# Routed rows of a mixture of experts written to their tokens' places by an indirect DMA per tile, in three groups of sequences

## The reference

```python
shared_out = einsum('tsh,shd->td', silu(xf @ sw1) * (xf @ sw3), sw2)
logits = xf @ router_w.T + experts_bias
rw, sel = top_k(logits, 2);  rw = softmax(rw)
cw = (one_hot(sel, 8) * rw[..., None]).sum(axis=1)
eo = silu(einsum('td,edh->teh', xf, w1)) * einsum('td,edh->teh', xf, w3)
moe_out = einsum('te,teh,ehd->td', cw, eo, w2)
x = layernorm(x + moe_out + shared_out)
```

## Time and profile before

| | us |
|---|---|
| median of 3 runs (615.56 to 618.25) | 616.53 |
| the profiled execution | 615.48 |
| its span | 613.5 |
| TensorE matmul, weight load busy | 500.8, 335.3 |
| VectorE busy | 467.0 |
| ScalarE busy | 313.0 |
| GpSimd busy | 323.5 |

### The profile page before, as it was taken

The page is one execution under the profiler, slowest core; times in us unless marked ns, Lnnn a source line. Parts: engine busy times, 40 slices in busy tenths (PEclk is TensorE's granted clock), DMA queues, the critical chain, the costliest instruction groups (busy, mean ns, idle before and its releaser), DMA issues.

```text
span 613.5 us, 14589 instructions
## 1 busy us (share of the span) xinstructions
PE 500.8 (82%) x4278; PEld 335.3 (55%) x4278; DVE 467.0 (76%) x1938; ACT 313.0 (51%) x752; POOL 323.5 (53%) x533
## 2 busy tenths in 40 slices
PE   6568889899879789999999989999899985497300
PEld 3212344456544249856675666767568984497200
DVE  3498999999978886998898999999826872165334
ACT  3106766766646645566666746575774432153100
POOL 5405634834668730268646765366865456405254
PEclk9786999999979789999999999999999998699755
DMA  5863322042526147744756483572456575697111
GB/s 167 230 199 113 115 80 80 3 130 80 165 72 191 57 127 210 247 144 140 230 166 188 128 238 104 139 212 90 127 149 183 159 215 142 183 306 244 39 52 51
DMA packets 77390, 90.40 MB, mean 147 GB/s; under 512 B 10241, under 2 KB 59393, under 8 KB 77313
## 3 DMA queue, kind: packets, MB, share of 16 engines
q1 hardware_dynamic: 69616, 78.79, 43.0%
q0 software_dynamic: 4096, 8.40, 4.6%
q10 hardware_dynamic: 3600, 2.30, 1.4%
HBM read 67.16 MB, written 21.89 MB: 145 GB/s over the span
## 4 chain that ended last, share of the span: by engine, by line
PE 55%; DVE 17%; issue 10%; POOL 4%; ACT 4%; DMA 4%; SPq 3%; another core or an unknown queue 2%; ACTq 0%; POOLq 0%; DVEq 0%
PE ps L1229 16%; PE ps L1135 10%; PE ps L1241 9%; PE ps L1091 8%; DVE sums L1311 6%; POOL yg L904 3%; PE ps L1077 2%; DVE acc L1459 2%; ACT probs L948 2%; PE ps L1146 2%; PE ps L1213 2%; DVE negmax L1311 1%; SPq L801 1%; PE ps L1084 1%
## 5 line engine op out<-in xcount | busy, mean ns | idle before, releaser
L1311 DVE CUSTOM_DVE_ANT_0 sums<-ps,mask_sb 128x384 bf16<-128x384 f32 (+3 forms) x512 | 218.0, 483 | 28.3 <-PE ps L1091 27.6
L948 ACT ACTIVATE probs<-ps 128x512 f32<-128x512 f32 x320 | 171.4, 610 | 54.5 <-PE ps L1091 44.9
L882 POOL TENSOR_SCALAR_AFFINE_SELECT probs<-probs 128x256 f32<-128x256 f32 (+1 forms) x320 | 113.0, 365 | 115.8 <-ACT probs L948 108.1
L1091 PE MATMUL ps<-stack 64*128 64x512 bf16 (+3 forms) x1024 | 120.2, 314 | 25.5 <-DMA stack<-parts_scratch 7.5
L1229 PE MATMUL ps<-xgT,w_tile 128*128 128x128 f32 x736 | 99.7, 284 | 0.8 <-ACT ot L984 0.6
L1436 DVE SCALAR_TENSOR_TENSOR gate<-th,ps 128x256 f32<-128x256 f32 x124 | 51.5, 416 | 63.3 <-ACT th L1012 55.8
L1229 PEld LDWEIGHTS ps<-xgT,w_tile 128*128 128x128 f32 x736 | 90.4, 196 | 9.1 <-issue 6.8
L904 POOL DMA_INDIRECT yg<-rows_out,slot x64 | 61.5, 961 | 60.2 <-DVE acc L1459 25.0
L1091 PEld LDWEIGHTS ps<-stack 64*128 64x128 bf16 x1024 | 42.7, 96 | 83.9 <-issue 21.2
L1135 PE MATMUL ps<-probs,va 128*32 128x512 f32 (+3 forms) x1024 | 84.0, 473 | 5.0 <-POOL probs L882 3.4
L894 POOL DMA_INDIRECT rows_in<-x,slot x64 | 63.0, 984 | 35.1 <-DVE slot L1428 23.9
(11 more groups left out here) (108 smaller groups left out, 582.6 us busy)
## 6 DMA issues: line engine op xcount, KB each, us to landing
w_tile<-in_experts SPq DMA_DIRECT2D x92, 384.0 KB
stack<-parts_scratch SPq DMA_DIRECT2D x106, 128.0 KB
parts_scratch<-parts SPq DMA_DIRECT2D x16, 384.0 KB
xg<-rows_in SPq DMA_DIRECT2D x20, 256.0 KB
rows_out<-y_routed SPq DMA_DIRECT2D x69, 64.0 KB
rows_in<-zeros SPq DMA_DIRECT2D x14, 192.0 KB, 3.8
x_t<-in_x SPq DMA_DIRECT2D x8, 256.0 KB, 3.0
x_r<-in_x SPq DMA_DIRECT2D x8, 256.0 KB
```

Of the source, the lines that this page charges most:

```text
L882: pool.affine_select(out=area, in_=area, compare_op=ALU.is_ge, fill=0.0, base=0, pattern=pattern, channel_multiplier=-1).then_inc(masked, 1)
L948: act.activation(probs[:, (s * NB + v) % PRING, :], bank("scores", s, v), ACT.Exp, scale=SCALE)\
L1091: return pe.matmul(into[:, at:at + width], here[:, stationary, at_s:at_s + P], here[:, moving, at_m:at_m + width], start=True, stop=True)
L1311: ins = dve.tensor_tensor_reduce(sums[:, use % 2, at:at + w], bank("max", s, u)[:, at:at + w], mask_sb[:, S - w:S], -1.0, 3.0e38, ALU.add, ...
```

## The change

Three groups, of three, three and two sequences: 31, 31 and 23 tiles. The scattered rows get two more columns: the place of the token and rank 0's expert. The sorted rows bring them back with each tile. `destinations` (VectorE, once per load of four tiles) compares the tile's expert with the row's first expert and so gets the row in `rows_out` where it belongs: token by token, both ranks side by side. `put_rows` then scatters each finished tile there with one indirect DMA from GpSimd's queue; padding rows have a place past the bound and are dropped. The stores from SP's and ScalarE's queues and the 64 gathers are gone. `load_y` fetches one sequence's 1024 rows (512 KB) with one plain DMA from SP's queue, once all puts of its group have landed and the combine before is done. There are seven weight buffers in place of eight, and the planner's tables are other ones: gaps between indirect DMAs go from 2600 and 1300 ns to 1300 and 1000, HOLD from 1000 to 500.

```diff
-SORTED = [[0, 1], [2, 3], [4, 5], [6, 7]]
+SORTED = [[0, 1, 2], [3, 4, 5], [6, 7]]
...
-GAP, GAP_LAST, GAP_END = 2600, 1300, 0
-HOLD = 1000
+GAPS = dict(scatter=(1300, 1000), put=(1000, 1000))
+HOLD = 500
...
-    XRING, WRING, YRING, HRING, TRING = 3, 8, 4, 3, 3
+    XRING, WRING, YRING, HRING, TRING = 3, 7, 4, 3, 3
...
+            if kind == "dest":
+                return [("sp", "load_rows", s, key[1])] + [("sp", "load_y", n) for n in (SORTED[s - 2] if s >= 2 else ())]
...
+            if kind == "put":
+                _, g, k = STEP[s]
+                found = [("act", "down", s), ("dve", "dest", g, k // XQ)]
+                return found + [("sp", "load_y", n) for n in (SORTED[g - 2] if g >= 2 else ())]
...
+        if kind == "load_y":
+            g = group_of[s]
+            found = [("pool", "put", step_of[("routed", g, k)]) for k in range(TILES[g])]
+            return found + [("dve", "combine", s - 1, T)]
...
-        x1 = sb("x1", [P, X1RING, T, D]); x1T = sb("x1T", [P, 2, S])
+        x1 = sb("x1", [P, X1RING, T, D + 2]); x1T = sb("x1T", [P, 2, S])
...
-        reached = sb("reached", [1, NT, E]); expert_f = sb("expert_f", [1, NT]); expert = sb("expert", [1, 2, NT], I32)
+        reached = sb("reached", [P, NT, E]); expert_f = sb("expert_f", [P, 2, NT]); expert = sb("expert", [1, 2, NT], I32)
...
-        def store_rows(eng, i):
...
-            eng.dma_start(rows_out[g % 2][k * P:(k + 1) * P, :], y_routed[:, use % YRING, :])\
-              .then_inc(rows_stored[use % YRING], 16)
...
+                    sp.wait_ge(dest_done, dest_use[(gone, qone)] + 1)
                     sp.wait_ge(*filled("T", gone, min(XQ * qone + XQ, TILES[gone]) - 1))
...
+            def load_y(s):
+                g = group_of[s]
+                for n in range(YRING):
+                    sp.wait_ge(rows_stored[n], 16 * stores_of(n, g))
+                if s > 0:
+                    sp.wait_ge(combined, s)
+                r0 = 2 * S * SORTED[g].index(s)
+                sp.dma_start(yg[:, :, :, :].rearrange("p t r d -> p t (r d)"),
+                             rows_out[g % 2][r0:r0 + 2 * S, :].rearrange("(t p r) d -> p t (r d)", p=P, r=2))\
+                  .then_inc(gathered[s % 2], 16)
...
-            def gather(g, s, t, r):
...
+            def put_rows(i):
...
+                pool.wait_ge(*drained("down", i))
+                pool.wait_ge(dest_done, dest_use[(g, k // XQ)] + 1)
+                if i == first_put[g] and g >= 2:
+                    for s in SORTED[g - 2]:
+                        pool.wait_ge(gathered[s % 2], 16 * (s // 2 + 1))
                 pool.indirect_dma_start(
-                    out=yg[:, t, r, :], out_offset=None, in_=rows_out[g % 2],
...
+                    out=rows_out[g % 2][0:count, :], out_offset=bass.IndirectOffsetOnAxis(ap=dest[:, g % 2, k:k + 1], axis=0),
+                    in_=y_routed[:, use % YRING, :], in_offset=None, bounds_check=count - 1, oob_is_err=False)\
+                    .then_inc(rows_stored[use % YRING], 16)
...
+                dve.tensor_copy(x1[:, s % X1RING, :, D], column["mark"][:, s * T:s * T + T])
+                dve.tensor_copy(x1[:, s % X1RING, :, D + 1], topf[:, :, 0])
...
+            def destinations(g, q):
...
+                dve.wait_ge(rows_here[use % XRING], 16 * (use // XRING + 1))
+                if g >= 2:
+                    for s in SORTED[g - 2]:
+                        dve.wait_ge(gathered[s % 2], 16 * (s // 2 + 1))
+                link(dve.tensor_tensor(same[:, 0:n], xg[:, use % XRING, 0:n, D + 1], expert_f[:, g % 2, XQ * q:XQ * q + n],
+                                       ALU.is_equal), dest_chain, 2 * done + 1)
+                link(dve.scalar_tensor_tensor(out=dest_f[:, 0:n], in0=same[:, 0:n], scalar=-1.0, in1=xg[:, use % XRING, 0:n, D],
+                                              op0=ALU.mult, op1=ALU.add), dest_chain, 2 * done + 2)
+                dve.tensor_scalar(dest[:, g % 2, XQ * q:XQ * q + n], dest_f[:, 0:n], float(past + 1), None, ALU.add)\
+                   .then_inc(dest_done, 1)
```

More of the change, by code:

```diff
@@ L395, in needs @@
                 rows = range(T) if key[1] == T else key[1:]
-                return [("pool", "gather", group_of[s], s, t, r) for t in rows for r in range(2)] + \
-                       [("pool", "shared_rows", step_of[("shared", s, t)]) for t in rows] + [("dve", "weights", s, 0)]
+                return [("sp", "load_y", s)] + [("pool", "shared_rows", step_of[("shared", s, t)]) for t in rows] + [("dve", "weights", s, 0)]
             if kind == "ln2_stats":
@@ L462, in length, with gap_of @@
         return round(taken), round(lasts)
+    def gap_of(part):
+        g = STEP[part[2]][1] if part[1] == "put" else part[2]
+        return GAPS[part[1]][g == len(SORTED) - 1]
     def plan():
@@ L505, in plan @@
                     continue
-                if kind in ("scatter", "gather"):
-                    after = GAP if part[2] < len(SORTED) - 1 else GAP_LAST if kind == "scatter" else GAP_END
+                if kind in GAPS:
+                    after = gap_of(part)
                     if now < indirect + after:
@@ L640, in build_block @@
         column = {}
[L641 removed]
+        for name, wide in (("earlier", P), ("ones", P), ("iota", E), ("thr", MOST), ("below", E), ("upto", E), ("tile", NT * E), ("mark", B * T)):
             column[name] = consts_sb[:, at:at + wide]
```

167 lines of the change are left out of this document (76 added, 91 removed), and 8 rows, old and new, of the table LATER.

## The result

The change makes the kernel slower: 641.7 us (640.7 to 646.4, four runs) against 617.0 us, a ratio of 1.042 (95% interval 1.036 to 1.047). The forecast was 599.6 us. The profiled execution took 640.7 us with a span of 638.9.

What follows compares the result with a forecast made beforehand. TensorE and VectorE bound the attention, then latency chains, last tiles and gathers. Last group's start 3.7 us earlier, last tiles equal, tail 12.2 shorter: span 613.5 - 15.9 = 597.6, so 599.6 us; range 585 to 616.

Steps and rivals of the forecast that it cites:

- the price of a put: TensorE idle per indirect DMA beside tiles: at most 0.16 us from 476 to 510 us, 0.54 where gathers are back to back.
- The attention: Up to the last output projection: 16 us from postponed tiles less 5 net, so 11 to 12 us earlier, at 464.
- forecast price of a tile: During attention, from 58 tiles in 50 us beyond five sequences' 240 us: 0.86 us a routed tile.
- the start: Kernel's start: more fills and tables cost 0 to 3 us, left at nothing in the sum.
- VectorE's new instructions: During attention: 0.6 us for each of 12 loads of sorted rows, 7 us, plus 3 us for two copies a sequence.
- The stretch behind the attention: Last output projection to last group's first tile: puts among scatters on GpSimd make it 8.4 us longer, first tile at 525.
- The last tiles: Last group's 23 tiles: 45 us kept; puts cost 3.7 us, set against 3.2 of gathers; clock near 1.0, some 2 us.
- The tail: Behind the last tile: put, two 512 KB loads, combines, norms and output take 27.3 in place of 39.5 us.
- C: Rival: indirect DMAs beside tiles hold TensorE's results, 0.54 us each, 626 us; decides from 0.46 us a put; chance 0.11.
- D: Rival: a put outlasts the tile period; at 1.9 + 0.3 us the last 23 tiles take 12.4 longer, 612; chance 0.04.
- wrong if above 474: Sign: sequence 7's last output projection near 464 us; above 474, VectorE or holds took the gain.
- Left at nothing: Effects priced at zero: rows of 520 bytes, one weight buffer less, SP's loads behind puts, more fills and tables.

Runs made afterwards that it cites:

- first kind: Three sets of runs in which the kernel before takes 616 to 619 us and traces show waits ended by "remote"; changed kernel 1.036 to 1.042 of it.
- second kind: Four sets of runs in which the kernel before takes 601 to 602 us and no trace shows a wait ended by "remote"; changed kernel 1.007 of it.
- Powers: Changed kernel, each of 85 puts replaced by a GpSimd power of four elements a partition, finished rows stored plainly in tile order: 0.974 of the kernel before, 599.8 us.
- plain: Changed kernel without its 85 puts, finished rows stored by plain DMAs from ScalarE's queue in tile order: 0.970 of the kernel before twice, 583.6 and 583.4 us.
- wide ones: Changed kernel, zero fills written as 1560 bytes a partition in place of 520-byte rows: 1.001 of the kernel before in one set, 1.029 in another.
- In pairs: Changed kernel with the earlier four groups of two sequences, 92 tiles and puts for 85: 1.054 of the kernel before, beside the unaltered 1.037.

## Why the prediction was wrong, point by point

The forecast was worked out on a trace of the first kind. Here are its stretches and what both kinds show. For the second kind the variant with 520-byte rows stands for the kernel before. "Powers" is the kernel with powers in the puts' place, "plain" the two runs with plain stores. Of the unaltered changed kernel the first measurement stands under the first kind; the run beside the powers has 489.0, 75.6, 47.7 and 25.9.

| us | before, forecast | first kind: before, changed, powers | second kind: before, changed, plain |
|---|---|---|---|
| to the last output projection | 475.9, 464 | 475.9, 489.0, 471.0 | 474.2, 469.9, 463.3 and 460.5 |
| from there to the last group's first tile | 52.7, 61 | 52.7, 75.2, 60.0 | 47.0, 61.9, 50.4 and 53.8 |
| from there to the last tile's result | 45, 45 | 45.1, 48.8, 44.1 | 38.4, 43.6, 43.3 and 43.3 |
| tail | 39.5, 27.3 | 39.8, 26.0, 23.9 | 39.8, 27.2, 23.9 and 23.9 |
| span | 613.5, 597.6 | 613.5, 638.9, 599.0 | 599.4, 602.5, 580.8 and 581.5 |

**The step that failed** is the price of a put beyond GpSimd's microsecond. The forecast took 0.16 us of TensorE for it, charged it to the last 23 puts alone (3.7 us, set off against the 3.2 us of the gathers), and put it at nothing for the other 62. The run with powers gives 0.47 us for each of the 85, 40 us. Between the two traces 39.2 us of span differ: 18.1 in the attention, 15.6 in the stretch behind it, 3.5 in the last tiles, 2.0 in the tail. So the holds cost about what was forecast in the last tiles, and nearly all of the loss lies where the forecast had nothing for them, among the scatters. With the powers the span is 599.0 us, and 597.6 was forecast. That this is so close is partly luck: the last output projection is 7 us later than forecast, and the tail 3.4 us shorter.

On the second kind, where nothing is held, the puts still cost 21.7 us, of which the forecast had the 8.4 of GpSimd's time behind the attention. There the change of the span is +3.1 us in place of -15.9.

**The attention (forecast 12 us earlier).** On the second kind it took 334.6 us from the second output projection to the last with 54 finished tiles, and takes 321.4 with 38, 13.2 less; 16 x 0.86 is 13.8. That looks like the forecast price of a tile, but the puts lie in it: with plain stores it is 316.4 and 311.0 us, 18 to 24 less. Two errors cancel, and what VectorE's new instructions cost was not measured apart. (The 58 tiles of the forecast are 57 transpositions and 54 finished tiles in the trace.) What failed as well is the start, for which I allowed 0 to 3 us: the second output projection stands at 148.5 in place of 139.7, of which the narrow fills are 2.7 (145.8 with wide ones). In pairs, with 16 fills in place of 22, it stands at 142.4 on the first kind, where the unaltered kernel has 149.3: much of the rest goes with the number of fills, as far as one plan can be compared with another. On the first kind the held results come on top, 19.1 us, more than half of them in one stage. The table of stages on the second kind, for the sequence with the 24 scatters and the two stages behind the attention, as those shown above; then these two stages in the kernel with 520-byte rows, in the second run with plain stores, and with powers (first kind):

```profile
356.00:429.00 73.00, 66.85 (x634) 50.41 (x634) 55.63 (x237) 41.28 (x105) 52.31 (x77) 0.98 0.47 140
...
470.00:531.70 61.70, 52.03 (x433) 50.23 (x433) 33.50 (x120) 23.32 (x81) 41.06 (x47) 0.92 0.66 198
531.70:575.40 43.70, 39.13 (x314) 36.77 (x312) 34.44 (x124) 19.66 (x73) 25.76 (x26) 0.96 0.82 268
```

```profile
474.20:521.30 47.10, 35.28 (x311) 33.62 (x309) 28.27 (x109) 16.78 (x56) 28.65 (x34) 0.93 0.72 211
521.30:559.80 38.50, 36.53 (x299) 34.94 (x299) 24.26 (x71) 19.03 (x69) 12.28 (x13) 0.96 0.80 249
```

```profile
460.60:514.30 53.70, 50.66 (x433) 49.15 (x433) 33.06 (x120) 23.78 (x81) 19.90 (x25) 0.97 0.73 219
514.30:557.90 43.60, 38.68 (x313) 36.82 (x312) 35.47 (x128) 20.87 (x73) 3.05 (x3) 0.96 0.91 296
```

```profile
471.00:530.90 59.90, 52.08 (x432) 49.99 (x433) 33.15 (x120) 23.94 (x81) 41.43 (x46) 0.94 0.66 197
530.90:575.40 44.50, 37.30 (x314) 35.27 (x312) 35.42 (x128) 20.79 (x73) 27.46 (x28) 1.00 0.88 289
```

The same work of the sequence with the scatters (633 and 634 matmul records) takes 73.0 us with a granted clock of 0.98 here and 84.2 with 0.90 on the first kind, and its matmuls 66.9 against 74.9: TensorE is stopped more often and is granted a lower mean clock. The forecast had nothing for either.

**The stretch behind the attention (forecast 8.4 longer, 61 us).** On the second kind 61.9 us, but against 47.0: 14.9 longer. GpSimd's part was right in kind. The last group's scatters, with puts between them:

```profile
490.20 0.98 POOL L898 DMA_INDIRECT rows_in<-x,slot  x1 [0.57 <-DVE slot L1436]
...
494.01 0.99 POOL L912 DMA_INDIRECT rows_out<-y_routed,dest  x1 [0.30 <-issue]
...
520.74 0.96 POOL L898 DMA_INDIRECT rows_in<-x,slot  x1 [0.30 <-issue]
```

9 puts lie between the 16 scatters: 31.5 us from first to last, against 20.0 without puts. What the forecast did not see is who waits behind this row on GpSimd: the addition for the shared expert, and through it ScalarE, VectorE and TensorE (above). On the first kind the stretch is 75.2 us, and 60.0 with the powers.

**The last tiles (forecast 45 us as before).** ScalarE's copies of finished tiles in the same two stages of the changed kernel on the second kind, in the table of stages for these instructions alone; then the second of them in the kernel with 520-byte rows:

```profile
470.00:531.70 61.70, 5.82 (x21) 0.92 0.66 198
531.70:575.40 43.70, 7.03 (x26) 0.96 0.82 268
```

```profile
521.30:559.80 38.50, 6.23 (x23) 0.96 0.80 249
```

The count of the forecast was nearly right: of the second group 24 tiles were left for the stretch behind the attention (forecast 23). 21 were finished there, and 3 were still under way when the last group's first tile came. 26 in place of 23 tiles lie in the last stage, and 3 x 1.66 = 5.0 of the 5.2 us by which it is longer (43.6 for 38.4). The puts cost nothing there: with plain stores it is 43.3 us. On the first kind the granted clock of this stage is 1.00, as I had expected, in place of 0.92.

Behind the last output projection TensorE does 91.2 us in place of 71.8 on the second kind and idles 14.2 in place of 13.8; with plain stores it idles 8 us. So part of the idle time that I had counted as room was room, as long as no puts stood among the scatters.

**The tail (forecast 27.3).** Right: 26.0 and 27.2 us. From the changed kernel's chain, the last put, its landing, and a load of 512 KB:

```profile
613.53 0.97 POOL rows_out L912
614.80 2.08 DMA rows_out<-y_routed,dest
616.89 3.46 DMA yg<-rows_out
```

The load took 3.4 to 3.5 us at the end and 4.84 beside other traffic at 582.62, for which 4.6 was taken. The 3.2 us by the fit of the Trainium skill ("DMA: Bandwidth & Descriptors", Anatomy of one DMA), which the page makes for DMAs issued from GpSimd while this load goes from SP's queue, were nearer at the end, where nothing else runs.

**The rivals.** C came true in its mechanism and its price, on the first kind: 0.54 us was taken and 0.47 measured, too near the threshold of 0.46 to be told from it. Its 626 us fell short of 641 because it charged the price to 49 indirect DMAs, the 37 that are more and 12 among the scatters, and not to all 85 puts. I gave it 0.11, since ten scatters in the earlier trace rows went with little idle time, and took the lower of two prices. The earlier trace rows had the other one, from indirect DMAs at 0.3 us from one another, and that is how the change issues many of its own. D did not show: no put took over 1.14 us. The sign "wrong if above 474" for the last output projection came with 489.0 us.

**Left at nothing.** The narrow fills cost 0.6%. The closer distances, which the forecast does not mention, cost 1.3 to 1.6% in the kernel before.

## What to carry to other kernels

Idle time of an engine in a stretch that is a chain of latencies is room for work only as long as the new work does not lengthen that chain, or stand in the same queue ahead of something that others wait for: here puts among the scatters held back an addition of a half microsecond, and TensorE stood for 7.6 us. An indirect DMA has two prices, GpSimd's microsecond and what it does to others who wait for TensorE; take the second from the places where they follow one another most closely, if the change will make them do so, and charge it to every one of them, not to those of one stage. And where a profile has waits that nothing explains, look whether another chip or another day has them too before pricing a plan by them.

## What the runs showed of the hardware

Results of TensorE reach ScalarE up to 9.7 us late while indirect DMAs are issued back to back, in three sets of runs; in the four others, with the same programs and indirect DMAs of the same length (0.98 us), no wait ends so, and the same tanh comes 0.04 us behind its matmuls. What differs between the sets stays open, as does what in an indirect DMA holds them. Puts replaced by powers of the same length took away 43 of 63 us of such waits and 40 us of time. For the kernel before the kinds are 2.5% apart (617 and 602 us), for the changed one 5.8% (640 and 605): the ratio of two kernels depends on it, 1.036 to 1.042 in one kind and 1.007 in the other.
